# Copies of k and q as two 512 KB transfers at chunk 6 in place of eight of 128 KB at chunks 1 and 5, and the inversion of the sums a chunk later

## What is computed

```python
xn = _layernorm(x, axis=-1)                       # x: 4 x 1024 x 128
normed = xn / l2 * dim ** 0.5 * gamma
qkv = (normed @ w_qkv).reshape(b, n, 3, h, d)     # 16 heads of 64
sim = einsum('bhid,bhjd->bhij', q * d ** -0.5, k)
sim = where(causal_mask, mask_value, sim)
attn = softmax(sim, axis=-1)
out = einsum('bhij,bhjd->bhid', attn, v) ... @ w_out
return x + attention(xn) + experts(xn)
```

## Time and profile before

| | |
|---|---|
| median of 3 runs | 1488.26 us (1487.44 to 1491.16) |
| the profiled execution | 1494.35 us, its span 1492.7 us |
| mean granted clock of PE in it | 0.95 |
| busy PE, DVE, ACT, POOL | 1323.4 us (89%), 963.3 (65%), 947.9 (64%), 896.6 (60%) |
| DMA | 107.66 MB, mean 72 GB/s |
| k_a<-k_a and q_b<-q_a | 128 transfers each, 128 KB each |
| tokens<-nT_dram | 32 transfers, 512 KB each |

### The profile page before, as it was taken

One profiled execution on the slowest core, in us unless ns is written; L12 is line 12 of the kernel. 1 busy time (PEld: TensorE's weight loads), 2 busy tenths in 40 slices (PEclk: granted clock), 3 DMA queues, 4 the chain that ended last, 5 costly groups with the idle time before them and its releaser, 6 DMA issues.

```text
span 1492.7 us, 27069 instructions
## 1 busy us (share of the span) xinstructions
PE 1323.4 (89%) x7880; PEld 1078.0 (72%) x7881; DVE 963.3 (65%) x2159; ACT 947.9 (64%) x2126; POOL 896.6 (60%) x1312
## 2 busy tenths in 40 slices
PE   4469989799859999999999999899999899999998
PEld 4446666799847777777777777777777777777777
DVE  5645644122245677778778777678678677778764
ACT  2425434455437777777777777677677777777775
POOL 3427651432226766767767766766766766866666
PEclk9679999899959999999999999999999999999999
DMA  5423221122222222323223223223223322322222
GB/s 199 171 69 90 70 72 63 53 75 77 61 61 60 58 64 69 70 62 76 61 62 75 66 58 71 66 65 68 62 59 73 70 58 67 78 58 58 60 58 71
DMA packets 169507, 107.66 MB, mean 72 GB/s; under 512 B 101240, under 2 KB 138144, under 8 KB 169376
## 3 DMA queue, kind: packets, MB, share of 16 engines
q1 hardware_dynamic: 148128, 72.65, 20.9%
q10 hardware_dynamic: 17152, 25.06, 5.7%
q0 software_dynamic: 4096, 8.40, 1.9%
HBM read 53.11 MB, written 18.86 MB: 48 GB/s over the span
## 4 chain that ended last, share of the span: by engine, by line
PE 45%; DVE 12%; DMA 7%; issue 5%; SPq 3%; ACT 2%; DVEq 0%; ACTq 0%
PE max_ps L1347 7%; DMA sums<-raw 7%; DVE max_ps L1181 6%; PE score_ps L1365 5%; PE score_ps L1364 5%; PE head_ps L1394 4%; PE head_ps L1392 4%; PE head_ps L1390 4%; PE misc_ps L1328 4%; PE head_ps L1385 4%; PE misc_ps L1405 3%; PE misc_ps L1320 2%; PE misc_ps L1322 2%; PE misc_ps L1321 2%; DVE stacked L1236 2%
## 5 line engine op out<-in xcount | busy, mean ns | idle before, releaser
L1061 POOL TENSOR_TENSOR p_lo<-probs,p_hi 128x512 fp32r<-128x512 f32 (+3 forms) x560 | 537.7, 961 | 176.0 <-ACT p_hi L1118 169.9
L1116 ACT ACTIVATE probs<-score_ps 128x512 f32<-128x512 f32 (+3 forms) x768 | 377.2, 491 | 258.5 <-PE score_ps L1365 253.5
L1181 DVE CUSTOM_DVE_ANT_0 max_ps<-max_ps,mask 128x128 f32<-128x128 f32 (+7 forms) x512 | 390.1, 764 | 160.4 <-PE max_ps L1347 152.3
L1364 PE MATMUL score_ps<-q_a,k_a 128*128 128x512 f32 (+3 forms) x768 | 308.5, 402 | 17.0 <-DMA q_b<-shift 16.9
L1347 PE MATMUL max_ps<-k_a,q_a 128*128 128x512 f32 (+3 forms) x768 | 241.4, 370 | 88.2 <-DVE shift L1181 82.7
L1053 POOL TENSOR_SCALAR_AFFINE_SELECT probs<-probs 128x128 f32<-128x128 f32 x512 | 174.8, 342 | 213.1 <-ACT p_hi L1118 148.2
L1365 PE MATMUL score_ps<-q_b,k_b 65*128 65x512 f32 (+3 forms) x768 | 271.8, 354 | 0.0
L1118 ACT ACTIVATE p_hi<-score_ps 128x512 fp32r<-128x512 f32 (+3 forms) x560 | 264.6, 472 | 0.0
L1347 PEld LDWEIGHTS max_ps<-k_a,q_a 128*128 128x128 f32 x768 | 141.2, 197 | 159.7 <-DVE shift L1181 76.4
L1385 PE MATMUL head_ps<-probs,v_all 128*65 128x128 f32 (+3 forms) x1088 | 252.6, 314 | 0.0
L1390 PE MATMUL head_ps<-p_hi,v_hi 128*65 128x512 f32 (+3 forms) x560 | 212.2, 379 | 0.2 <-POOL p_lo L1061 0.2
(11 more groups left out here) (170 smaller groups left out, 2096.6 us busy)
## 6 DMA issues: line engine op xcount, KB each, us to landing
tokens<-nT_dram ACTq DMA_DIRECT2D x32, 512.0 KB, 5.0
k_a<-k_a SPq DMA_DIRECT2D x128, 128.0 KB
q_b<-q_a SPq DMA_DIRECT2D x128, 128.0 KB
rden_all<-inverse_row SPq DMA_DIRECT2D x60, 256.0 KB, 3.6
q_b<-shift SPq DMA_DIRECT2D x512, 0.5 KB
sorted_x<-zeros SPq DMA_DIRECT2D x13, 384.0 KB, 5.3
rows<-sorted_x SPq DMA_DIRECT2D x39, 128.0 KB, 2.1
sorted_y<-result ACTq DMA_DIRECT2D x39, 128.0 KB, 1.9
```

The lines of the kernel that those rows point to most:

```text
L1061: pool.tensor_tensor(p_lo[:, lo_slot(W, c), w0:w1], probs[:, slot, w0:w1], p_hi[:, slot, w0:w1].bitcast(F32), ALU.subtract).then_inc(pool_ ...
L1116: ins = act.activation(probs[:, slot, 0:width], src[:, 0:width], ACT.Exp, scale=SCALE)
L1181: dve.tensor_tensor_reduce(out=max_ps[:, at:at + width], in0=max_ps[:, at:at + width], in1=mask[:, SEQ - width:SEQ], scale=-1.0, scalar=-M ...
L1364: pe.matmul(dst, k_a[i][s][:, keys], q_a[i][s][:, qs], start=True, stop=False)
```

## The change

q_a, k_a, q_b and k_b get the two heads of a pair as a dimension of one tile, so that 8 KB of a row lie together. `copies` waits for the last high part of the pair and issues two transfers; it has a place of its own in the list, behind chunk 6 of the even unit. Only the first pair of each attention keeps copies by half (two transfers of 256 KB for each). What finishes a unit moves by a chunk: the inversion from 8 to 9, its store from 10 to 11, the spread from 0 to 1, the two products from 3 and 4 to 4 and 5, the projection of the output from 7 and 9 to 8 and 10. The load of tokens moves from chunk 7 to chunk 9. In the first unit of an attention the next pair's projections 0 to 3 go from chunks 0, 1, 3, 5 to 2, 3, 3, 5.

```diff
-            q_a = [[sb(ph2, f"q_a{i}{s}", [P, SEQ], F32R) for s in range(2)] for i in range(2)]
+            q_a = [sb(ph2, f"q_a{i}", [P, 2, SEQ], F32R) for i in range(2)]
...
-            PROJECT_AT = [{0: 0, 1: 1, 3: 2, 5: 3}, {1: 4, 5: 5}]
+            PROJECT_AT = [{0: (0,), 1: (1,), 3: (2,), 5: (3,)}, {1: (4,), 5: (5,)}]
+            FIRST_PROJECT_AT = {2: (0,), 3: (1, 2), 5: (3,)}
...
-            Y_AT = {7: 0, 9: 1}
+            Y_AT = {8: 0, 10: 1}
...
                     if stacks(W - 1):
-                        order += [(kind, W - 1, 0) for kind, at in (("sums", 5), ("invert", 8), ("inverse", 10))
+                        order += [(kind, W - 1, 0) for kind, at in (("sums", 5), ("invert", 9), ("inverse", 11))
                                   if at == c]
                     if stacks(W - 2):
-                        order += [(kind, W - 2, n) for kind, n, at in (("spread", 0, 0), ("norm", 0, 3),
-                                                                      ("norm", 1, 4)) if at == c]
+                        order += [(kind, W - 2, n) for kind, n, at in (("spread", 0, 1), ("norm", 0, 4),
+                                                                      ("norm", 1, 5)) if at == c]
...
-                    if W % 2 == 0 and c == 7 and W // 2 + 1 < QL:
+                    if W % 2 == 0 and c == 6 and W // 2 + 1 < QL:
+                        order.append(("copies", W // 2 + 1, 0))
+                    if W % 2 == 0 and c == 9 and W // 2 + 1 < QL:
                         order.append(("tokens", W // 2 + 1, 0))
...
-                    def copies(Q, half):
-                        cols = slice(half * BANK, (half + 1) * BANK)
-                        sp.wait_ge(hi_done, Q * 8 + 4 + half * 4)
-                        for s in range(2):
-                            k_hi, q_hi = k_a[Q % 2][s][0:HEAD, cols].bitcast(F32), q_a[Q % 2][s][0:HEAD, cols].bitcast(F32)
-                            sp.dma_start(k_a[Q % 2][s][HEAD:P, cols].bitcast(F32), k_hi).then_inc(copies_done[half], 16)
-                            sp.dma_start(q_b[Q % 2][s][0:HEAD, cols].bitcast(F32), q_hi).then_inc(copies_done[half], 16)
+                    def copies(Q):
+                        i = Q % 2
+                        sp.wait_ge(hi_done, Q * 8 + 8)
+                        sp.dma_start(k_a[i][HEAD:P].bitcast(F32), k_a[i][0:HEAD].bitcast(F32)).then_inc(copies_done, 16)
+                        sp.dma_start(q_b[i][0:HEAD].bitcast(F32), q_a[i][0:HEAD].bitcast(F32)).then_inc(copies_done, 16)
...
                     for kind, g, c in order:
-                        if kind == "project" and c in (1, 3):
-                            copies(g, c // 2)
+                        if kind == "project" and g == Q0 and c in (1, 3):
+                            first_copies(c // 2)
                         if kind == "shift":
                             shifts(g, c)
+                        if kind == "copies":
+                            copies(g)
...
-                            pe.wait_ge(copies_done[half], Q * 64 + 64)
+                            if Q == Q0:
+                                pe.wait_ge(first_copied[half], 32 if native else 64)
+                            elif half == 0:
+                                pe.wait_ge(copies_done, n_copies(Q) * 32)
```

More of the change, by code:

```diff
@@ L717, in attention_and_experts @@
         pool_split = sem("pool_split")
-        copies_done = [sem(f"copies_done{i}") for i in range(2)]
+        copies_done = sem("copies_done")
+        first_copied = [sem(f"first_copied{i}") for i in range(2)]
         shift_done = [sem(f"shift_done{i}") for i in range(2)]
@@ L748, in attention @@
             tokens = sb(ph2, "tokens", [P, SEQ])
[L749 to L752 removed]
+            q_a = [sb(ph2, f"q_a{i}", [P, 2, SEQ], F32R) for i in range(2)]
+            k_a = [sb(ph2, f"k_a{i}", [P, 2, SEQ], F32R) for i in range(2)]
+            q_b = [sb(ph2, f"q_b{i}", [HEAD + 1, 2, SEQ], F32R) for i in range(2)]
+            k_b = [sb(ph2, f"k_b{i}", [HEAD + 1, 2, SEQ], F32R) for i in range(2)]
             v_all = [sb(ph2, f"v_all{i}", [P, TILES, 2, HEAD + 1]) for i in range(2)]
@@ L847, in beside @@
                     order += [("max", *item) for item in max_items(W, c)]
-                    if c in PROJECT_AT[W % 2] and W // 2 + 1 < QL:
-                        order.append(("project", W // 2 + 1, PROJECT_AT[W % 2][c]))
-                        order.append(("project_lo", *order[-1][1:]))
+                    for n in (FIRST_PROJECT_AT if W == W0 else PROJECT_AT[W % 2]).get(c, ()):
+                        if W // 2 + 1 < QL:
+                            order += [(kind, W // 2 + 1, n) for kind in ("project", "project_lo")]
                     if W % 2 and c in Y_AT and stacks(W - 2):
@@ L853, in beside @@
                     if W == WL - 1 and c in LAST_Y_AT:
-                        order += [(kind, W - 1, LAST_Y_AT[c]) for kind in ("last_y", "last_add")]
+                        order += [(kind, W - 1, n) for n in LAST_Y_AT[c] for kind in ("last_y", "last_add")]
                     if c:
@@ L933, in shifts @@
                     def shifts(W, t):
-                        row = q_b[W // 2 % 2][W % 2][HEAD:HEAD + 1, t * P:(t + 1) * P]
+                        row = q_b[W // 2 % 2][HEAD:HEAD + 1, W % 2, t * P:(t + 1) * P]
                         sp.wait_ge(max_taken, n_max(W, t) + 1)
@@ L1346, in max_scores_of @@
                             k1 = min(width, k0 + BANK)
-                            ins = pe.matmul(max_ps[:, at + k0:at + k1], q_a[i][s][:, t * P:(t + 1) * P],
-                                            k_a[i][s][:, k0:k1], start=True, stop=True)
+                            ins = pe.matmul(max_ps[:, at + k0:at + k1], q_a[i][:, s, t * P:(t + 1) * P],
+                                            k_a[i][:, s, k0:k1], start=True, stop=True)
                         ins.then_inc(max_scores, 1)
@@ L1363, in score @@
                             pe.wait_ge(shift_done[half], (W + 1) * 16 * HALF_TILES)
-                        pe.matmul(dst, k_a[i][s][:, keys], q_a[i][s][:, qs], start=True, stop=False)
-                        pe.matmul(dst, k_b[i][s][:, keys], q_b[i][s][:, qs], start=False,
+                        pe.matmul(dst, k_a[i][:, s, keys], q_a[i][:, s, qs], start=True, stop=False)
+                        pe.matmul(dst, k_b[i][:, s, keys], q_b[i][:, s, qs], start=False,
                                   stop=True).then_inc(scores_ready, 1)
```

19 lines of the change are left out of this document (13 added, 6 removed).

## The result

| | before | after |
|---|---|---|
| median of 4 runs each, side by side | 1489.71 us | **1567.61 us** (1567.02 to 1568.62) |
| ratio | | 1.0523 (95% interval 1.0502 to 1.0544) |
| span of the profiled execution, granted clock | 1492.7 us, 0.95 | 1565.3 us, 0.94 |
| busy DVE | 963.3 us | 1029.2 us |

The change makes the kernel 78 us slower. The forecast was 1443, its range 1420 to 1475: wrong in size and in direction. 1560, rival C's number, is near, but its mechanism is not what happened.

A forecast was written before the change was run, and what follows sets the result against it. PE sets the time, broken by waits in which a small DMA (sums) ends last. Terms 44 + 10 + 12 - 18 - 3 = 45 us less: 1449 us for the profiled execution, 1443 against the median, range 1420 to 1475.

The forecast's parts named there:

- rival C: Odd unit's start: 8 KB rows run at half rate, copies land late and PE waits; 1560 us, chance 0.08.
- Step 4: Even units: norm products move to after maximum 4, still ahead of maximum 5; no change in time.
- Step 8: Odd units: second norm product now behind v_lo, ahead of maximum 5; costs 3 us, ends 0 and 11.
- Step 9: Later inverse, spread, products and output projection, and shifts of tiles 5 to 7 behind copies; all at nothing.
- Steps 1 and 2: Odd units: sums no longer behind copies on SP; 44.4 us less in second attention, 10 us in first.
- Step 3: First unit of each attention: shifts for score chunk 4 no longer behind copies; 12 us less, ends 4 and 17.
- Steps 6 and 7: Copies land by the odd unit's start, cost 0; tokens two chunks later make PE wait, cost 18 us.
- Rivals A, B and D: Tokens: A in time, 1422 us, 0.16; B 1 us later, 1470 us, 0.16; D wait eats gain, 1488 us, 0.05.
- Step 5: SP's issues: eight of 0.6 us become two per pair; worth nothing alone.

The follow-up runs named there:

- e3: Changed kernel with only the spread (chunk 0) and the two norm products (chunks 3 and 4) put back; 1496.6 us.
- e10: e6 with only the norm products moved to chunks 4 and 5 and the spread to chunk 1; 1529.9 us.
- e8: Changed kernel with GpSimd's p_lo cut to 32 columns and PE's third product reading p_hi instead; 1487.0 us.
- e7: e3 with GpSimd's p_lo cut to 32 columns and PE's third product reading p_hi instead; 1481.6 us.
- e1: Changed kernel with the finishing part (inversion, its store, spread, norm products, output projection) placed as before; 1481.2 us.
- e12: e9 with the inversion, its store and the output projection each a chunk later; 1470.1 us.
- e9: e6 with the last five gathers of the combine steps at chunks 0 to 4 instead of 1, 3, 5, 7, 9; 1449.5 us.
- e5: e1 with the load of tokens back at chunk 7 instead of 9; 1500.6 us.
- e6: e5 with a semaphore of its own for the copy of q, awaited a unit later; 1459.9 us.

## Why the prediction was wrong

*Step 4 failed*, and with it the sign. "The norm products go from before and after maximum 4 to after it, both still ahead of maximum 5: same work, same end." The order was read rightly, the work was not the same: both products fell on p_lo and took 1.4 us each. The even units are 50.6 us longer than before, and 53.5 longer than e3's, where the products stand at their old places. e10 prices the move at 70 us by itself, e8 against e7 at 5 us without p_lo.

*Step 8* named the right place and was mis-sized: 0.15 to 0.2 us in 16 odd units, 3 us, ends 0 to 11. PE waits 1.8 us there in unit 37 (the next matmul, at 1033.20), since the step behind the product is held too. Over all 26 odd units the changed kernel takes 17.8 us more than e3, which has the products back. Even the upper end, the product's 0.69, was too low, because it took the other rows' durations as fixed.

*Step 9* put the rest at nothing; moving the inversion and the projection costs 15 us (e3 against e1) to 21 us (e12 against e9), and perhaps less in the changed kernel, whose spread moves along. rden_all was in time there, as said (11.9 us in 2 waits, 9.2 in 2 before).

*Steps 1 and 2*: the mechanism was right (no wait for sums is left), but 44.4 us asked that nothing else be late in the same place. In e1 tokens were, in e5 the copies, in e6 the gathers; only e9 brings 500.7 - 468.2 = 32.5 us of it, and its even units take 7.2 us more than before. In the changed kernel units 3 and 5 of the first attention gave 2.4 and 1.6 us of the 10, and unit 1 lost 2.3.

*Step 3* held: the two first units went from 32.86 to 28.23 and from 33.02 to 27.30 us, 10.4 us for my 12. PE no longer waits for a shift before score chunk 4 in either.

*Steps 6 and 7*: I had the copies landed 4.0 to 5.1 us behind 939.3 and their price at 0. In e1, behind an issue at 969.51, PE is let go at 976.67, 7.2 us later: my rates were right (212 and 196 GB/s in this stretch) but I took the first of two issues as the start of all, and 1.05 MB as all that moves. The row of the windows also shows the 16 DMA engines full, with a share of 1.01, at the 212 GB/s; rival C had them not even full at 206:

```profile
970.50:973.60 3.10, 1.96 (x12) 1.35 (x10) 2.27 (x6) 1.38 (x3) 2.70 (x4) 1.00 1.01 212
```

Tokens I had at 0.6 us x 30 = 18; e1 has 28.7 us in 26 waits, the changed kernel 9.4 in 5. Its slower even units leave more time between the first copy and tokens, 6.2 us in unit 36 (1009.56 and 1015.76) against 4.2 in e1 (969.51 and 973.66); that this is the reason is my reading, not tested. The fit of the Trainium skill that step 7 sets beside the rows (DMA: Bandwidth & Descriptors, anatomy of one DMA) is measured for DMAs that GpSimd issues, and tokens are issued by ACT. Rivals A, B and D spoke of tokens alone. Rival C's wait, PE at the first maximum for the copies, is real (8.8 us in e1, 47.2 in e5), but not in the changed kernel, whose even units were slow enough to hide it.

*Step 5*, SP's issues at nothing, has nothing against it.

## What to carry to other kernels

Before an instruction is moved at no cost, look at what the other engines do at its new place in the trace: two rows of the same instruction at 0.68 and at 1 us or more are a sign that a neighbour decides its length. When a wait is taken away, list what else is needed at that moment and by how much it is early; here three transfers stood behind the one, with 27 to 47 us of waits each. A semaphore that two transfers share makes the first user wait for both: giving each its own was worth 40.7 us.

## What was not expected of the hardware

A VectorE instruction of 128x4 took 1.12 us beside a p_lo of GpSimd, against 0.15 us apart from it; 512 columns of fp32 took 1.41 against 0.68. The tile gvar, its line L124, in the changed kernel and in e7 (count: ns min/median/max):

```profile
L124 DVE SCALAR_TENSOR_TENSOR gvar<-gvar x24: 151/730/1123, 537.5 to 1418.9; 128x4 f32<-128x4 f32 x24
```
```profile
L124 DVE SCALAR_TENSOR_TENSOR gvar<-gvar x24: 144/152/157, 534.9 to 1344.2; 128x4 f32<-128x4 f32 x24
```

Over all 24 the median is 730 ns in the changed kernel, 238 before and 152 in e7. The wait also goes the other way: GpSimd's mask of the diagonal, 0.29 us as a rule, took 0.75 beside a product (changed kernel, unit 36), and the p_lo at 1030.68 above, which began while a product was running, took 1.51 us against 1.28:

```profile
1009.10 0.75 POOL L1070 TENSOR_SCALAR_AFFINE_SELECT probs<-probs 128x128 f32<-128x128 f32 x1
```

Over the whole program, DVE's work in e7 with the short p_lo is 89 us less than in e3 (992.9 and 1082.0 us, summed over its instructions), for the same instructions.
